# Four transformer layers as three jobs of a sequence, maxima turned by VectorE, and an order that keeps tilings

## The reference

```python
# layer 0: self attention (rotary, block mask), cross attention, MLP, each gated
# layer 1: cross attention alone; the context is normalised and modulated too; biases
# layer 2: self attention (bias, gate), cross attention (context normalised), MLP (gate)
# layer 3: self attention (rotary), cross attention (rotary), MLP (exact gelu)
def _attn(q, k, v):
    scores = jnp.einsum('bqhd,bkhd->bhqk', q, k) * scale
    w = jax.nn.softmax(scores, axis=-1)
    return jnp.einsum('bhqk,bkhd->bqhd', w, v)
def _mlp(x):
    h = jax.nn.gelu(x @ W1 + b1)       # 256 -> 1024
    return h @ W2 + b2                 # 1024 -> 256
```

## Time and profile before

| | us |
|---|---|
| median of 3 runs | 2992.43 (2983.66 to 2996.97) |
| the profiled execution, device time | 2985.79 |
| its span, first to last instruction | 2984.0 |
| TensorE busy | 2822.5 (95%) |
| VectorE busy | 1846.7 (62%) |
| ScalarE busy | 1486.9 (50%) |
| mean granted TensorE clock | 0.97 |

### The profile page before, as it was taken

The page is one execution under the profiler, slowest core; times in us unless marked ns, Lnnn a source line. Parts: engine busy times, 40 slices in busy tenths (PEclk is TensorE's granted clock), DMA queues, the critical chain, the costliest instruction groups (busy, mean ns, idle before and its releaser), DMA issues.

```text
span 2984.0 us, 58003 instructions
## 1 busy us (share of the span) xinstructions
PE 2822.5 (95%) x21570; PEld 2049.1 (69%) x21570; DVE 1846.7 (62%) x4668; ACT 1486.9 (50%) x2329; POOL 288.1 (10%) x340
## 2 busy tenths in 40 slices
PE   6889999999999899988899999999989999999999
PEld 5556766766777766665676777777657777776777
DVE  2577556666664466675655757576567767767652
ACT  0334645544545455435356454545655565464654
POOL 0000101000001211101111111111000000000000
PEclk9899999999999999988799999999989999999999
DMA  4444324333432466643534343434235333333320
GB/s 134 151 143 152 110 72 143 112 112 102 129 115 82 152 177 188 204 131 98 177 99 128 106 148 108 146 108 149 78 111 176 115 108 123 112 123 118 122 74 18
DMA packets 279147, 369.41 MB, mean 124 GB/s; under 512 B 32458, under 2 KB 158218, under 8 KB 278556
## 3 DMA queue, kind: packets, MB, share of 16 engines
q1 hardware_dynamic: 246620, 318.63, 35.5%
q10 hardware_dynamic: 32256, 47.07, 4.3%
HBM read 224.49 MB, written 110.97 MB: 112 GB/s over the span
## 4 chain that ended last, share of the span: by engine, by line
PE 71%; DVE 14%; DMA 5%; ACT 3%; issue 3%; SPq 1%; POOL 0%; ACTq 0%; DVEq 0%; POOLq 0%
PE gen L1209 11%; PE gen L1067 10%; PE gen L1158 9%; PE gen L1200 8%; PE gen L1032 8%; DVE row_max L1497 7%; PE score L1133 4%; PE score L1109 3%; PE score L1080 3%; PE gen L1169 3%; PE gen L1041 2%; PE score L1095 2%; PE score L1139 2%; DMA parts_scratch<-parts 2%; PE gen L1118 2%
## 5 line engine op out<-in xcount | busy, mean ns | idle before, releaser
L1319 ACT ACTIVATE probs<-score 128x1024 f32<-128x1024 f32 (+1 forms) x576 | 570.2, 1024 | 365.6 <-PE score L1133 221.1
L1497 DVE TENSOR_REDUCE row_max<-score 128x4 f32<-128x1024 f32 (+1 forms) x640 | 650.5, 1048 | 154.9 <-PE score L1095 96.9
L1200 PE MATMUL gen<-xnT,w_w 128*128 128x256 f32 x1536 | 367.9, 386 | 3.0 <-ACT hT L1341 1.8
L1209 PE MATMUL gen<-w_w,hT 128*128 128x256 f32 x1536 | 354.1, 384 | 4.1 <-ACT hT L1341 2.3
L1351 POOL TENSOR_TENSOR rstd<-var_eps,minus_half 128x2 f32<-128x2 f32 x160 | 113.0, 707 | 2317.1 <-DVE var_eps L1394 2316.1
L1209 PEld LDWEIGHTS gen<-w_w,hT 128*128 128x128 f32 x1536 | 284.4, 190 | 53.4 <-issue 12.6
L1200 PEld LDWEIGHTS gen<-xnT,w_w 128*128 128x128 f32 x1536 | 282.2, 191 | 49.7 <-issue 9.6
L1326 ACT COPY oT<-gen 128x512 f32<-128x512 f32 x224 | 131.3, 589 | 251.2 <-PE gen L1158 246.7
L1341 ACT ACTIVATE hT<-gen,b_b 128x256 f32<-128x256 f32 x384 | 160.2, 473 | 150.7 <-PE gen L1200 149.8
L1264 ACT ACTIVATE xnT<-gen,mod_all 128x256 f32<-128x256 f32 x288 | 147.0, 568 | 151.8 <-PE gen L1041 151.6
L1095 PE MATMUL score<-k_self,q_stack 64*128 64x256 f32 x1536 | 191.8, 342 | 28.0 <-DVE row_max L1497 15.4
(11 more groups left out here) (138 smaller groups left out, 4276.8 us busy)
## 6 DMA issues: line engine op xcount, KB each, us to landing
q_stack<-parts_scratch SPq DMA_DIRECT2D x336, 256.0 KB, 3.7
parts_scratch<-parts ACTq DMA_DIRECT2D x160, 256.0 KB, 2.6
parts_scratch<-parts SPq DMA_DIRECT2D x160, 256.0 KB, 2.8
k_self<-parts_scratch SPq DMA_DIRECT2D x144, 256.0 KB, 4.2
q_stack<-zeros_scratch SPq DMA_DIRECT2D x112, 256.0 KB, 3.9
q_stack<-maxT SPq DMA_DIRECT2D x224, 128.0 KB, 2.7
k_cross<-parts_scratch SPq DMA_DIRECT2D x192, 78.0 KB, 2.5
x_scratch<-x SPq DMA_DIRECT2D x48, 256.0 KB, 3.2
```

What stands on the lines that cost most here:

```text
L1200: mm = pe.matmul(buf[:, i * S:i * S + S], w["w1"][:, fc, col:col + P], xnT[s][:, fc, :], start=fc == 0, stop=fc == FC - 1)
L1209: mm = pe.matmul(buf[:, 0:D], hT[:, j, c * P:c * P + P], w["w2"][:, j, :], start=j == 0, stop=j == FFC - 1)
L1319: act.activation(probs[st.probs][0:keys, :, :], score[st.fill.buf][0:keys, :, :].rearrange("p a (r q) -> p (a r) q", r=2), ACT.Exp, bias=k ...
L1497: dve.tensor_reduce(dst, src, AX_X, ALU.max).then_inc(max_done[b], 1)
```

## The change

The second and the third layer become one job of four blocks for each sequence (48 jobs). The three areas of attention weights A, B and C rotate over the blocks; C lies partly over the two masks, which only the first layer's self blocks read. The maxima are turned by VectorE in blocks of 32 x 32; the steps `mT` and `mc` are gone. The transposed context lies in a ring of two. A context load waits for the block before its own, and the stores of a context block's parts wait for the transfers of the slot's cross block before. The order counts 12 for a job's age in place of 8, and gives 4 to a TensorE step whose tiling is the one that is set. The sums of the reciprocals (`rsum`) share a tile with the maxima.

```diff
-MAXIMA = 3
+MAXIMA = 2
+CTX_T = 2
 LAYERS = [
-    Layer("L0", 1e-5, P, 0, 3, 0, 3, [
-        Block("self", mod=0, rope=True, mask=True, gate=0),
...
+    [Block("L0", "self", "A", 1e-5, mod=0, rope=P, mask=True, gate=0),
+     Block("L0", "cross", "B", 1e-5, mod=1, gate=1, mask=True, ctx="raw"),
+     Block("L0", "mlp", "M", 1e-5, mod=2, gate=2, out_bias=True, gelu="tanh")],
+    [Block("L1", "cross", "C", 1e-5, mod=3, qk_bias=0, out_bias=True, ctx="norm", ctx_mod=4, behind=(0, 0)),
+     Block("L2", "self", "A", 1e-6, mod=5, qk_bias=2, out_bias=True, gate=3),
+     Block("L2", "cross", "B", 1e-6, qk_bias=4, out_bias=True, ctx="norm"),
+     Block("L2", "mlp", "M", 1e-6, mod=6, gate=4, out_bias=True, gelu="tanh")],
+    [Block("L3", "self", "C", 1e-5, mod=7, rope=S),
+     Block("L3", "cross", "A", 1e-5, mod=8, rope=S, ctx="raw"),
+     Block("L3", "mlp", "M", 1e-5, mod=9, out_bias=True, gelu="erf")],
 ]
...
-            "mx": 0.36, "mT": 0.22, "mc": 0.33,
+            "mx": 0.92,
...
-            before = [i for i in range(li) if blk.kind in LAYERS[i].kinds]
-            users = [self.ends[before[-1] * B + seq, blk.kind] for seq in range(B)] if before else []
+            before = blk.behind or max(((i, n) for i in range(li + 1) for n in range(len(LAYERS[i]))
+                                        if (i, n) < (li, k) and LAYERS[i][n].area == blk.area), default=None)
+            users = [self.ends[before[0] * B + seq, before[1]] for seq in range(B)] if before else []
...
-            ctx = add("ldc", 0, "sp", [])
+            ctx = add("ldc", 0, "sp", [early])
...
             mx = add("mx", h, "dve", maxima[h * n:h * n + n])
-            mT = add("mT", h, "pe", [mx])
-            mc = add("mc", h, "dve", [mT], mT)
-            spread = [add("sd", h, "sp", [mc])]
+            spread = [add("sd", h, "sp", [mx])]
...
-                st = min(can, key=lambda st: (8 * st.job - st.rank, 0))
+                st = min(can, key=lambda st: (12 * st.job - st.rank - 4 * (eng == "pe" and TILES.get(st.name, "whole") == self.tiles), 0))
...
-        max_tok = [sb(f"max_tok{i}", [P, TC, P], F32R) for i in range(MAXIMA)]
+        max_tok = [sb(f"max_tok{i}", [P, TC, 4 * PAIRS], F32R) for i in range(MAXIMA)]
...
+        w["C"] = {"q": maskk[:, :, :].bitcast(F32), "kv": sb("w_kvC", shapes["kv"]), "out": maskq[:, :, :].bitcast(F32)}
...
-        maxT = [sb(f"maxT{i}", [P, S], F32R) for i in range(MAXIMA)]
+        maxT = [sb(f"maxT{i}", [4 * PAIRS, TC, P], F32R) for i in range(MAXIMA)]
-        rsum = per_slot("rsum", [P, TC, H])
+        rsum = row_max
...
+                    if st.k:
+                        sp.wait_ge(*moved(step[st.job, st.k - 1, "xT", 0]))
                     sp.dma_start(ctx_in[buf][:, :], a["ctx"][st.seq]).then_inc(ctx_loaded[buf], 16)
...
+                    if way(st) == 2 and st.nth_way > 1:
+                        sp.wait_ge(*placed_before(st))
...
-                    sp.wait_ge(*moved(of(st, "mT", h)))
+                    sp.wait_ge(max_turned, of(st, "mx", h).nth_all)
...
-                    ins.then_inc(max_tok_ready, 1)
-
-                def maxima_moved(st):
...
+                    link(ins)
+                    for b in range(P // 32):
+                        ins = dve.transpose(maxT[st.got["max"]][:, :, 32 * b:32 * b + 32].bitcast(F32),
+                                            max_tok[st.got["max"]][32 * b:32 * b + 32, :, :].bitcast(F32))
+                    ins.then_inc(max_turned, 1)
```

More of the change, by code:

```diff
@@ L179, in rings_of @@
         takes += ("ctx_in",)
+    if name == "cT":
+        takes += ("ctxT",)
+    if name == "qkv" and j == 2 and not blk.whole:
+        gives += ("ctxT",)
     if name == "cT":
@@ L236, in job_steps @@
         kept = self.ends.get((job - SLOTS, "stx"))
-        last = self.add(job, 0, first, "ldx", 0, "sp", [self.ends.get((job - B, "stx"))])
+        last = early = self.add(job, 0, first, "ldx", 0, "sp", [self.ends.get((job - B, "stx"))])
         gate_free = left
-        for k, blk in enumerate(layer.blocks):
-            ready = self.weights[li, blk.kind]
+        for k, blk in enumerate(layer):
+            ready = self.weights[li, k]
             def add(name, j, eng, after, fill=None):
@@ L253, in job_steps @@
             else:
-                last = self.attention_steps(add, blk, job, xe, [xb, gate, None if k else kept], ready)
-            self.ends[job, blk.kind] = last
+                last = self.attention_steps(add, blk, job, xe, [xb, gate, None if k else kept], ready, early)
+            self.ends[job, k] = last
+            early = xe
             gate_free = last if gate else gate_free
@@ L259, in job_steps @@
         self.ends[job, "job"] = last
-        self.ends[job, "stx"] = self.add(job, len(layer.blocks) - 1, blk, "stx", 0, "sp", [last])
+        self.ends[job, "stx"] = self.add(job, len(layer) - 1, blk, "stx", 0, "sp", [last])
     def mlp_steps(self, add, xe, xb, ready):
@@ L270, in mlp_steps, with attention_steps @@
         return last
-    def attention_steps(self, add, blk, job, xe, ready_x, ready):
+    def attention_steps(self, add, blk, job, xe, ready_x, ready, early):
         def high_and_low(j, fill):
@@ L278, in high_and_low @@
             none = add("zq", j, "sp", [xe]) if j == 0 else None
-            return [add("lh", j, "sp", [add("ph", j, "act", [high]), none]), add("ll", j, "sp", [add("pw", j, "sp", [low]), none])]
+            before = () if blk.whole or j == 0 else self.ends.get((slot, "context"), ())
+            loads = [add("lh", j, "sp", [add("ph", j, "act", [high, *before]), none]), add("ll", j, "sp", [add("pw", j, "sp", [low, *before]), none])]
+            if not blk.whole and j:
+                self.ends[slot, "context"] = loads
+            return loads
+        slot = f"slot{job % SLOTS}"
         if blk.whole:
@@ L288, in attention_steps @@
         else:
-            before = self.ends.get((job - SLOTS, "qkv2"))
-            ctx = add("ldc", 0, "sp", [])
+            ctx = add("ldc", 0, "sp", [early])
             if blk.ctx == "norm":
@@ L297, in attention_steps @@
             keys = high_and_low(1, qkv)
-            qkv = self.ends[job, "qkv2"] = add("qkv", 2, "pe", [ce, ready, qkv])
+            qkv = add("qkv", 2, "pe", [ce, ready, qkv])
             value = add("ve", 2, "dve" if blk.qkv_bias else "act", [qkv], qkv)
@@ new lines, in bias_tile, with out_bias_of, weights_loaded @@
+        def bias_tile(blk, key):
+            return bias[key + "1" if blk.of == "L1" else key]
+        def out_bias_of(blk):
+            return bias_tile(blk, {"self": "so", "cross": "co", "mlp": "b2"}[blk.kind])
+        counted, loads_through = dict.fromkeys(AREAS, 0), {}
+        for blocks in LAYERS:
+            for blk in blocks:
+                counted[blk.area] += 16 * len(weight_dmas(blk))
+                loads_through[blk] = counted[blk.area]
+        def weights_loaded(blk):
+            return w_loaded[blk.area], loads_through[blk]
@@ L848, in cross_of, with context_of @@
             return of(st, "qkv", 1).got["cross"]
+        def context_of(st):
+            return of(st, "cT").got["ctxT"]
         def own(st):
```

214 lines of the change are left out of this document (94 added, 120 removed).

## The result

The kernel after takes 2948.14 us (median of 4 runs, 2936.06 to 2956.18), the one before 2988.05 beside it: ratio 0.9865, 95% interval 0.9839 to 0.9892. That is 40 us less, where 167 were forecast, and outside the range of 2755 to 2900. The profiled execution took 2956.18 us, its span is 2954.4.

What follows compares the result with a forecast made beforehand. TensorE, 95% busy, was taken as the bound, with idle time and low clock around layer borders. Gains 67 + 90 + 18 - 5 - 3 = 167 us off 2985.8, with 6.6 for the median, gave 2825 us; range 2755 to 2900.

Steps and rivals of the forecast that it cites:

- (a): Transposes of the maxima leave TensorE: 224 steps and their tiling changes, a gain of 67 us.
- (c): TensorE's order prefers the set tiling and older jobs: fewer entries into 64-row runs, half of 35 us, gain 18 us.
- (b): Layer borders, 969 to 2238 us: merged jobs and rotating weight areas win back 90 of 118 us lost.
- (d): VectorE turns the maxima itself: 52 us more VectorE work, priced by its 14% chain share, net cost 5 us.
- (e): Smaller maxima ring, later context loads and store guards on the queues: together a cost of 3 us.
- Rival A: Two remaining layer borders cost 29.4 us each, with windows near them showing TensorE under 90%: 2869 us; chance 0.13.
- The sign that did come: Clock of the windows: no window behind 300 us was to be below 0.95.
- The share of 0.14: VectorE's 14% of the chain that ended last, used as the price of its added time.
- The ends on the bad side: Whole kernel: all terms at their unfavourable ends, a gain of only 45 us, 2947 us.
- Rival C: 64-row score steps: tiling preference makes TensorE wait for a third score buffer, 176 us, 3001 us; chance 0.04.

Runs made afterwards that it cites:

- f2: The kernel before with the order rule alone (12 for a job's age, 4 for the set tiling): 2953.9 us, ratio 0.9885.
- e3: The kernel after with the maxima transposed by TensorE and copied by VectorE again (rule, areas and merge stay): 2923.5 us, ratio 0.9784 to before.
- h3: The kernel before with the order rule and the maxima turned by VectorE, neither areas nor merge: 2934.2 us, ratio 0.9840.
- e1: The kernel after with second and third layer as separate jobs again (rule, turn and areas stay): 2893.1 us, ratio 0.9677 to before.
- f4: The kernel after without the merge and with the maxima on TensorE again (rule and areas stay): 2935.1 us, ratio 0.9819 to before.
- h2: e3 with 190 us of idle work (fills of an unused tile) added to VectorE: 2994.7 us, ratio 1.0041 to before.
- i2: The kernel after with three context buffers and the maxima step planned at 1.48 us in place of 0.92: 2911.0 us, ratio 0.9746 to before.
- h4: e1 with the age weight of 12 but no advantage for the set tiling: 3069.2 us, ratio 1.0295 to before.

## Why the prediction was wrong

| step | forecast | measured |
|---|---|---|
| (a) mT off TensorE, (c) its tiling changes: TensorE's work | -85 | -79, from busy x clock |
| (b) merge and areas | -90 | -30 (f2 to e3) with maxima on TensorE; +14 (h3 to after), not clear of noise, with the turn |
| (c) the rule as a whole | -18 | -33 alone, -71 on e1 |
| (d) VectorE's added time | 52 us | 176 us |
| (d) price of one us of it | 0.14 | 0.14 to 0.84 for the turn itself, 0.37 to 0.65 for idle work |
| (e) rings and queues | +3 | not separated; with a third context buffer -15 |

The whole miss can be followed along one path of runs: before to f2 (rule) gains 33 us, f2 to e3 (areas and merge) 30, e3 to after (turn) loses 25; together 38 of the 40 us measured. The sum had 18 for the rule, 87 for areas and merge with (e), and 62 for the turn, (a) less (d). So the turn is 87 us worse than forecast, the merge with the areas 57, and the rule 15 better. Another path would share out the parts otherwise, as they act on each other.

**(a) and (c), TensorE's work: right.** The 448 transposes are gone, and 69 us of busy time. The kernel after has 759 runs of 64-row steps for the 834 of before; the 737 that half of (c)'s way down would be were not reached, and the rule's gain is more than its changes of tiling.

**(b) failed.** "So the border inside 1044 to 1492 us is gone altogether" held for the late weights, but the loss was not their wait. (b) kept 13 us for the 555 us of work around the borders and nothing for the third layer's 596 us, as if any mixture of jobs would run like the steady stretches of one layer. From 900 to 2088 us the kernel after lost 149 us, e3 68, and e1 93, each with its third layer's weights fetched earlier than before. Together with the turn and the areas, the merge costs 55 us (e1 to after); without the turn it gains 12 (f4 to e3), within the noise. Rival A, borders that stay, did not come: no window of its sign is under 92% busy, the last border is closed, and its 2869 us was still too low. The sign that did come is a window below clock 0.95: 1492 to 2088 us at 0.94.

**(d) was mis-sized twice.** Transposes don't overlap as the two small operations at 334.69 do, and the whole step has a negation, a split, a wait on its own result and four transposes, 1.49 us in all. And the share of a chain isn't the price of an engine's time. What the turn takes, with (a)'s 67 us added back: 81 + 67 = 148 us for 176 on the kernel before, 47 with the rule, 57 with the areas, 25 with both, 92 in merged jobs. The sum had 5, and its upper end was 34. With the 92 of merged jobs in place of the 5 the forecast would have been 2912; with the 0.37 that e3's load shows, 176 x 0.37 = 65 us and 2885. The share of 0.14 fits rule and areas (25 of 176) by luck: the same way of pricing misses the other four by a factor of about two to six.

**Slips in the sum.** The ends on the bad side add up to 55 + 45 - 34 - 20 = 46 us, not 45. With the 2 us that (d) gives back, the 150 cycles of the Trainium skill, "VectorE: DVE Perf Modes", section on the TRN2 errata, would make the sum 11 us worse by estimate, not 13. The 81 ns of the Trainium skill, "TensorE: Matmul & The Clock Gate", section Back-to-back issue gap, would take 60.5 - 36 = 24 us off the gain by estimate, not 30. None of these matters to the result.

**Rival C** as written did not come. TensorE's longest sums of waits in the kernel after (us, times, longest) have 52 us for row maxima at three score lines, 62 over all, far from 100:

```profile
PE gen L1071 <- DVE xhat L1421: 24.3, 18, 12.3
PE score L1124 <- DVE row_max L1518: 23.1, 34, 2.2
PE gen L1201 <- DVE xhat L1547: 21.9, 28, 1.9
PE score L1160 <- DVE row_max L1518: 15.3, 19, 2.3
PE score L1109 <- DVE row_max L1518: 13.5, 19, 2.9
```

Beside them stand 46 us for the normalised x (`xhat`) of blocks that begin, which VectorE gives behind whatever its list holds. Both kinds are waits for VectorE, an engine that is busy two thirds of the time: it is late at places in its list, not full.

**What stays open.** Why merge and turn together cost 55 us. It is not the count of tiling changes (759 runs of 64-row steps in the kernel after, 760 in e1), and 12 more table loads of 1.283 us on ScalarE are too few by themselves. Idle work on VectorE costs less in merged jobs, not more (h2), but the turn costs more there. 37 us of it go with two edits that move no work between engines (i2). Orders with the same work for TensorE and VectorE lie up to 176 us apart (e1, h4), so a part of each difference above may be the luck of one order; no run averages over orders, and none keeps ScalarE's table loads fixed. The old rule finds no order for merged jobs, so rule and merge were not taken apart there.

## What to carry to other kernels

Before moving work to an engine that is not the bound, don't price it by its share of the chain. At 62% busy, with lists in fixed order, one microsecond of idle work cost 0.37 to 0.65 us here, and one of the moved work 0.14 to 0.84. Idle work is a warning and not a price: it put the three kernels in another order than the moved work did. Where the order is written out ahead of time, time it with its steps' measured costs, and try its weights in pairs, since each alone can do nothing or harm (2964, 2962 and 3069 against 2893 us); then count what the order changed besides, here ScalarE's table loads. Before taking a hole for a wait, look at what the engine waits for in it. A hole that is closed at a border is only a gain if the work that fills it isn't taken from a stretch that had none.

## What the hardware showed

- Four transposes of 32 x 64 f32 by VectorE take 0.97 us at 421.75, where the forecast had 0.55.
- Two transposes of 128 x 128 f32 by TensorE take 0.27 us from start to start in the kernel before.
- A load of a function table by ScalarE takes 1.283 us each time, 104 of them in e1_split and 218 in h4_split12.
- Where TensorE waited more, its clock was lower: with the same TensorE instructions in all, h4_split12 is busy 91% of the last layer's stretch at 0.92 where e1_split is busy 97% at 0.99. The first row is h4's, the second e1's:

```profile
2088.00:2800.00 712.00, 648.40 (x4582) 469.14 (x4581) 491.31 (x1268) 361.84 (x547) 44.80 (x54) 0.92 0.35 109
```

```profile
2088.00:2800.00 712.00, 691.06 (x5282) 514.37 (x5281) 543.60 (x1413) 388.03 (x610) 47.75 (x58) 0.99 0.39 119
```
